# Latent attention on one core: a second bank for the single units, and the turned probabilities in three pieces through two banks

## The chip, the cores and the metric

The kernel runs on one core of a Trainium2 chip. The metric is device time in microseconds of one launch. The engines are PE (TensorE: matmuls and transposes), DVE (VectorE), ACT (ScalarE), POOL (GpSimd) and SP (SyncE, here only DMA). Each works through its own instructions in program order; semaphores tie them together. PE writes its results to PSUM, eight banks of 512 fp32 columns on 128 partitions, from which DVE and ScalarE read.

## The reference, cut to what matters

The whole program is a block of residual layers on x of 4 x 512 x 256: a small mixture with low-rank experts, a first attention, the small mixture again, a mixture of 32 experts, then the **latent attention**, and the mixture of 32 experts once more. The change is in the latent attention alone:

```python
qc = rms_norm(x @ wq_down, q_norm_w)              # 96 columns
q_nope, q_pe = (qc @ wq_up), (qc @ wq_rope)       # 16 heads of 128 and of 64
kvc = rms_norm(x @ wkv_down, kv_norm_w)           # 64 columns
k_nope, v = split(kvc @ wkv_up)                   # 16 heads of 128 and 128
k_rope = x @ wk_rope                              # 64, shared by the heads
q_pe, k_rope = apply_rope(q_pe), apply_rope(k_rope)
scores = einsum('bqhd,bkhd->bhqk', q, k) * scale
probs = softmax(scores + causal_mask)
out = einsum('bhqk,bkhd->bqhd', probs, v).reshape(4, 512, 16 * 128)
return out @ wo
```

## The kernel before, in words

`latent_stage` (L1229 on) handles B = 4 batches of H1 = 16 heads, 64 heads in all, in a software pipeline of STEPS = 66 **steps** S. Each engine has its own loop over S, written by hand; nothing but these loops and the semaphores sets the order. Weights are folded beforehand, so that a head's query has 128 columns and a batch's keys are shared by its heads.

In step S the engines do, in this order:

- **PE** (L1411 on): `scores(S, 0)`, the largest block of the scores of head S (128x512 and a mask product) into its bank of psA; `queries(S + 2)`, the query of the head after next (96x512, L1346) into psU; `scores(S, 1)` and `(S, 2)`, the other blocks; in odd steps from 3 on `values`, the product of the turned probabilities of heads S-3 and S-2 into psO (L1381); a **side unit**, if the step has one; `turn(S - 1)`, which transposes the ten 128x128 blocks of the causal probabilities of head S-1 into psP (L1371).
- **DVE**: `maxima(S, 0)` (L1607); `queries(S + 2)`, which reads the query from psU, multiplies it with the cosines (L1595) and twice with the sines (L1599) and then frees psU; the other maxima; `divide(S, 0..2)`, which turns the exponentials into probabilities (L1614, L1617); then what the step has besides.
- **ScalarE**: the four exponentials of head S (L1469), each group when its maxima are there; in odd steps from 3 on the copy of psO (L1478); the copy of the side unit; the copy of the turned probabilities of head S-1 from psP to prT, 128x1280 in one instruction (L1486).
- **POOL** adds the two parts of the query and stores rows for the experts; SP loads.

The **side units** are single products or transposes of the neighbouring batches: in steps 6 and 7 of a batch (S modulo 16) the turned rows of the next batch ("x"), in 8 and 9 the down product ("d", of which ScalarE also takes the sums of squares, L1447 and L1451), in 13 the turned query rows ("qT"), in 14 and 15 the keys ("k"), and in 2 to 5 the output product of the batch before ("o": sixteen matmuls in L1340 of eight pairs, added to x by DVE in L1662). Queries and side units together are the **single units**. They share one bank, psU, and one semaphore, u_free: unit n begins when unit n-1 has been read out.

DVE's further work lies in fixed steps: added rows of the experts' result (2.04 us in L1563, in steps 0 to 3, 6, 8, 11, 14, 17, 20, 24, 28), the layer norm of the next batch's rows in step 5 of a batch, its norms in step 10, and for the batch before statistics, scales and normal rows in steps 6, 7 and 8. A **bare** step is one with none of all this.

PSUM before: psA three banks (scores), psP three banks, of which 1280 columns are used, psU one, psO one: all eight. The places in psP and prT (BT) and the two places where the banks are given back:

```python
BT = {0: 0, 1: 512, 3: 896, 2: 1024}
...
def unit(key):
    if u_index[key] >= 1:
        pe.wait_ge(u_free, u_index[key])
...
def turn(h):
    if h >= 1:
        pe.wait_ge(pT_ready, h)
    for k, ts in enumerate(BANKS):
        pe.wait_ge(quotient, NBK * h + k + 1)
```

Of the kernel before, what the change touches and what calls it, by code (L numbers as in the profile page):

```python
# [18 lines left out]
P = 128  # L19
# [1209 lines left out]
def latent_stage(nc, block, sem_of, stored, r, ident, la, slot, rows_dram, placed, spare, picks, half_weight, out_dram, reloads, experts_in):  # L1229
# [5 lines left out]
    BT = {0: 0, 1: 512, 3: 896, 2: 1024}  # L1235
    NS = 1280
# [31 lines left out]
    with ExitStack() as ctx:  # L1268
# [3 lines left out]
        def sem(n):  # L1272
# [26 lines left out]
        (dstep, pstep, u_ready, u_free, xn_ready, ss_ready, kv_ready, kn_ready, q_part, q_ready, a_done, nb_ready,  # L1299
         exp_done, quotient, turned, pT_ready, v_done, o_copied, out_done, ptick, xd_ready) = (sem(n) for n in (  # L1300
             "dstep", "pstep", "u_ready", "u_free", "xn_ready", "ss_ready", "kv_ready", "kn_ready", "q_part", "q_ready",
             "a_done", "nb_ready", "exp_done", "quotient", "turned", "pT_ready", "v_done", "o_copied", "out_done",
             "ptick", "xd_ready"))
        outs, OPENS = [psU[:, 0:D], psU[:, D:2 * D], psA[:, 0:D], psA[:, 512:512 + D]], (0, 2, 3)
# [3 lines left out]

        @block.tensor
        def _(pe):  # L1310
            def unit(key):
                if u_index[key] >= 1:
                    pe.wait_ge(u_free, u_index[key])

            def side(key):
                kind, b, n = key
                unit(key)
                if kind == "x":
                    pe.wait_ge(xn_ready, TPB * (b + 1))
                    for j in range(TPB):  # L1320
                        ins = pe.transpose(psU[:, j * P:(j + 1) * P], xn[:, j * D + n * P:j * D + (n + 1) * P], ident[:, :])
                elif kind == "d":
                    for e in range(2):
                        j = 2 * n + e
                        for k in range(KD):
                            ins = pe.matmul(psU[:, e * ND:(e + 1) * ND], xT[:, k * L + j * P:k * L + (j + 1) * P],
                                            la.down[:, k * ND:(k + 1) * ND], start=(k == 0), stop=(k == KD - 1))
                elif kind == "qT":
                    pe.wait_ge(kv_ready, b + 1)
                    for j in range(TPB):  # L1330
                        ins = pe.transpose(psU[0:QR, j * P:(j + 1) * P], qn[:, j * QR:(j + 1) * QR], ident[:, :])
                elif kind == "k":
                    pe.wait_ge(kn_ready, b + 1)
                    o = 0 if n else 64
                    for j in range(TPB):
                        ins = pe.transpose(psU[:, j * P:(j + 1) * P], kn[b % 2][:, j * 192 + o:j * 192 + o + P], ident[:, :])
                else:
                    pe.wait_ge(o_copied, PAIRS * (b + 1))
                    for c in range(PAIRS):
                        ins = pe.matmul(psU[:, 0:D], oT[(b * PAIRS + c) % RING][:, n * P:(n + 1) * P], la.vo[:, c * D:(c + 1) * D],  # L1340
# [3 lines left out]
            def queries(h):  # L1344
                unit(("q", h))
                pe.matmul(psU[:, :], la.qw[:, h % H1 * P:(h % H1 + 1) * P], qT[h // H1 % 2][:, :], start=True,  # L1346
                          stop=True).then_inc(u_ready, 1)

            def scores(h, k):
                if k == 0:  # L1350
                    pe.wait_ge(q_ready, h + 1)
                if k == 0 and h % H1 == 0:
                    pe.wait_ge(u_free, u_index[("k", h // H1, 1)] + 1)
# [10 lines left out]
            def turn(h):  # L1364
                if h >= 1:
                    pe.wait_ge(pT_ready, h)
                for k, ts in enumerate(BANKS):
                    pe.wait_ge(quotient, NBK * h + k + 1)
                    for qt in ts:
                        for kt in range(qt + 1):  # L1370
                            ins = pe.transpose(psP[:, BT[kt] + (qt - kt) * P:BT[kt] + (qt - kt + 1) * P],  # L1371
                                               pr[h % 2][:, AT[qt] + kt * P:AT[qt] + (kt + 1) * P], ident[:, :])
                ins.then_inc(turned, 1)

            def values(g):
                pe.wait_ge(pT_ready, 2 * g + 2)
# [28 lines left out]
            pe.wait_ge(u_free, u_index[("q", 0)])  # L1405
            for h in range(2):
                queries(h)
            for S in range(STEPS):
                if S < HEADS:
                    scores(S, 0)  # L1410
                    if S + 2 < HEADS:  # L1411
# [7 lines left out]
                if 1 <= S <= HEADS:  # L1419
                    turn(S - 1)  # L1420
                if S == HEADS - 1:
                    pe.wait_ge(u_free, len(order))
# [15 lines left out]
        def _(act):  # L1438
            def side(key):
                kind, b, n = key  # L1440
                made(act, key)
                if kind == "x":
                    act.copy(xT[:, n * L:(n + 1) * L], psU[:, :]).then_inc(u_free, 1)
# [391 lines left out]
```

## Time and profile before

| | |
|---|---|
| median of 3 runs | 1489.26 us (1489.18 to 1489.72) |
| profiled execution, its own time | 1499.06 us |
| span of its trace | 1497.0 us |
| mean granted clock of PE in it | 0.934 |
| latent stage within the span | about 700 to 1255 us |
| the 64 turned copies (L1486) | 1.23 us each, from 751.7 to 1244.7 us |

The profiled execution is 9.8 us longer than the median; its durations are used for the working, and sums are made against its own time. In the rows, a time in front is the start in us from the start of the span, then the length in us, the engine and the line. A bracket at the end is how long the engine sat idle before it, and what released it. "x10" is a number of merged instructions. Ends of matmuls are modelled and overlap with the next; the distance of two starts on PE is what a piece costs.

### The profile page before, as it was taken

What the parts mean: (1) busy time and instruction counts of PE and PEld (TensorE: products, weight loads), DVE (VectorE), ACT (ScalarE), POOL (GpSimd) and SP (SyncE); (2) the same over time, 40 slices, a digit from 0 to 9 for tenths busy, and PEclk for the clock granted to TensorE, in tenths of its full rate; (3) what the DMA queues carried; (4) which work ended last, traced back from release to release, by engine and by line L of the source; (5) the groups of instructions that cost most, each with busy time, mean ns of one, the idle gap of its engine ahead of it and who ended that gap; (6) DMA issues with size and microseconds to landing.
All of it is one profiled execution on the core that took longest, in us unless ns stands there. A gap on an engine that the chain in (4) does not pass through costs nothing.

```text
span 1497.0 us, 22302 instructions
## 1 busy us (share of the span) xinstructions
PE 1267.1 (85%) x6633; PEld 816.1 (55%) x6634; DVE 950.7 (64%) x2721; ACT 671.1 (45%) x1706; POOL 502.9 (34%) x495
## 2 busy tenths in 40 slices
PE   6769898898888599998778889889889997899980
PEld 4514243343336578887545455556546556788870
DVE  6786758777756622224498978887897793123227
ACT  2205655555672055553245444453554461255540
POOL 2054040052315645552111211351152153355550
PEclk7959998999999699999999999999999998899995
DMA  7527543073304166554011100020010112344538
GB/s 283 108 25 117 179 85 42 1 150 147 151 19 162 72 231 203 181 166 152 3 54 29 29 1 1 11 103 1 7 36 15 57 43 102 102 157 156 164 124 280
DMA packets 78687, 147.91 MB, mean 99 GB/s; under 512 B 11693, under 2 KB 60014, under 8 KB 75758
## 3 DMA queue, kind: packets, MB, share of 16 engines
q1 hardware_dynamic: 62782, 104.36, 24.8%
q0 software_dynamic: 15360, 41.96, 7.8%
q8 instruction: 60, 0.98, 0.3%
q14 instruction: 53, 0.43, 0.1%
q10 hardware_dynamic: 432, 0.17, 0.0%
HBM read 83.15 MB, written 62.91 MB: 98 GB/s over the span
## 4 chain that ended last, share of the span: by engine, by line
PE 54%; DVE 27%; issue 7%; ACT 6%; POOL 3%; DMA 2%; another core or an unknown queue 0%; SPq 0%; DVEq 0%; POOLq 0%; ACTq 0%
PE m_psG L1164 12%; PE m_psY L1180 5%; DVE a_t L1599 4%; DVE a_mx L852 4%; PE a_psO L456 3%; PE m_psX L1155 3%; DVE a_nb L1607 3%; PE a_psA L1358 3%; PE a_psU L431 3%; PE a_psU L1340 3%; PE a_psW L397 2%; ACT a_pr L1469 2%; POOL rows_dram L166 2%; PE a_psS L442 2%; DVE x L1134 2%
## 5 line engine op out<-in xcount | busy, mean ns | idle before, releaser
L166 POOL DMA_INDIRECT outs_dram<-m_ys,dest x192 | 184.5, 961 | 162.8 <-ACT m_ys L1099 129.8
L1469 ACT ACTIVATE a_pr<-a_psA,a_nb 128x512 f32<-128x512 f32 (+3 forms) x256 | 132.8, 525 | 218.5 <-DVE a_nb L1607 218.0
L1119 DVE TENSOR_TENSOR m_hm<-m_psG,m_sg 128x128 f32<-128x128 f32 x192 | 56.0, 292 | 266.5 <-ACT m_sg L1093 159.2
L852 DVE TENSOR_REDUCE a_mx<-a_psU 128x1 f32<-128x512 f32 x256 | 163.7, 684 | 67.4 <-PE a_psU L431 65.5
L1164 PE MATMUL m_psG<-arena,m_xgT 128*128 x768 | 202.2, 386 | 2.2 <-ACT m_xgT L1087 1.6
L1525 POOL TENSOR_TENSOR a_q<-a_q,a_t 64x512 f32<-64x512 f32 x64 | 80.8, 1263 | 353.3 <-DVEq L1602 329.4
L166 POOL DMA_INDIRECT rows_dram<-a_xd,slot x128 | 139.3, 1089 | 165.3 <-DVE a_xd L146 78.4
L587 ACT ACTIVATE a_P<-a_psS 128x512 f32<-128x512 f32 x256 | 142.7, 597 | 50.8 <-PE a_psS L442 44.7
L1164 PEld LDWEIGHTS m_psG<-arena,m_xgT 128*128 128x128 f32 x768 | 130.6, 190 | 19.0 <-issue 7.1
L1607 DVE TENSOR_REDUCE a_nb<-a_psA 128x1 f32<-128x512 f32 (+3 forms) x256 | 113.3, 485 | 34.9 <-PE a_psA L1360 24.3
L431 PE MATMUL a_psU<-arena 96*128 96x512 bf16 x256 | 106.7, 419 | 32.8 <-DVE a_mx L852 30.7
L1180 PE MATMUL m_psY<-arena,m_hT 128*128 x384 | 115.0, 382 | 0.1
L1087 ACT COPY m_xgT<-m_psX 128x256 f32<-128x256 f32 x192 | 72.4, 378 | 83.5 <-PE m_psX L1155 83.5
L442 PE MATMUL a_psS<-arena 108*128 108x512 bf16 x256 | 97.8, 388 | 9.3 <-ACT a_P L587 7.7
L1358 PE MATMUL a_psA<-arena,a_q 128*128 128x512 f32 (+3 forms) x256 | 91.3, 466 | 16.5 <-ACT a_pr L1469 15.8
L1617 DVE TENSOR_SCALAR a_pr<-a_pr,a_rec 128x512 f32<-128x512 f32 (+3 forms) x256 | 97.1, 401 | 6.8
L1099 ACT COPY m_ys<-m_psY 128x256 f32<-128x256 f32 x192 | 71.5, 372 | 59.0 <-PE m_psY L1180 34.6
L1486 ACT COPY a_prT<-a_psP 128x1280 f32<-128x1280 f32 x64 | 79.1, 1236 | 42.0 <-PE a_psP L1371 41.9
L1358 PE MATMUL a_psA<-a_kT,a_q 128*128 128x512 f32 (+3 forms) x256 | 88.1, 453 | 9.4 <-ACT a_pr L1469 7.6
L1093 ACT ACTIVATE m_sg<-m_psG 128x128 f32<-128x128 f32 x192 | 53.6, 279 | 86.2 <-PE m_psG L1164 75.6
L1599 DVE TENSOR_TENSOR a_t<-a_psU,la_sin 32x512 f32<-32x512 f32 x128 | 87.9, 687 | 1.7
L431 PEld LDWEIGHTS a_psU<-arena 96*128 96x128 bf16 x256 | 25.5, 100 | 111.8 <-DVE a_mx L852 87.9
(270 smaller groups left out, 2319.2 us busy)
## 6 DMA issues: line engine op xcount, KB each, us to landing
m_xg<-rows_dram SPq DMA_DIRECT2D x46, 512.0 KB
arena<-in_mo_w SPq DMA_DIRECT2D x9, 2048.0 KB
arena<-part_dram SPq DMA_DIRECT2D x96, 128.0 KB
arena<-outs_dram SPq DMA_DIRECT2D x16, 512.0 KB, 3.9
rows_dram<-a_P SPq DMA_DIRECT2D x6, 1024.0 KB, 14.1
part_dram<-a_part SPq DMA_DIRECT2D x16, 384.0 KB, 5.3
rows_dram<-arena SPq DMA_DIRECT2D x6, 1024.0 KB, 15.5
m_xg<-outs_dram SPq DMA_DIRECT2D x8, 512.0 KB, 4.6
```

What stands on the lines that cost most here:

```text
L166: pool.indirect_dma_start(out=rows_dram, out_offset=bass.IndirectOffsetOnAxis(ap=slot[:, c:c + 1], axis=0), in_=row, in_offset=None).then_ ...
L431: pe.matmul(psU[n % 2][:, :], QS[0:NT, o + h * L + qt * P:o + h * L + (qt + 1) * P], KS[0:NT, o + h * L:o + (h + 1) * L], start=True, stop ...
L442: pe.matmul(psS[n % 2][:, :], KS[0:KC, o + h * L + kt * P:o + h * L + (kt + 1) * P], QS[0:KC, o + h * L:o + (h + 1) * L], start=True, stop ...
L587: act.activation(Pr[:, o:o + L], psS[c % 2][:, :], ACT.Exp).then_inc(exp_done, 1)
L852: dve.tensor_reduce(mx[g % 2][:, 4 * kt + qt:4 * kt + qt + 1], psU[n % 2][:, :], AX, ALU.max).then_inc(u_free, 1)
L1164: ins = pe.matmul(psG[b % 2][:, 0:2 * INTER], xgT[:, (b % 2) * D + k * P:(b % 2) * D + (k + 1) * P], GU[:, ds(e * (KD * 2 * INTER) + k * 2 ...
L1180: pe.matmul(psY[m % 2][:, 0:D], hT[:, (m % 2) * P:(m % 2 + 1) * P], DW[:, ds(e * D, D)], start=True, stop=True).then_inc(y_done, 1)
L1358: pe.matmul(psA[:, AT[t]:AT[t] + (t + 1) * P], qh[:, t * P:(t + 1) * P], kh[:, 0:(t + 1) * P], start=True, stop=False)
L1469: ins = act.activation(pr[S % 2][:, AT[t]:AT[t] + (t + 1) * P], psA[:, AT[t]:AT[t] + (t + 1) * P], ACT.Exp, bias=nb[S % 2][:, t:t + 1], sc ...
L1599: ins = dve.tensor_tensor(t2[to:to + 32, o:o + L], psU[lo:lo + 32, :], la.sin[lo:lo + 32, :], ALU.mult)
L1607: ins = dve.tensor_reduce(nb[s % 2][:, t:t + 1], psA[:, AT[t]:AT[t] + (t + 1) * P], AX, ALU.max, negate=True)
L1617: ins = dve.tensor_scalar(pt, pt, rec[s % 2][:, t:t + 1], None, ALU.mult)
```

## The change

psP becomes two banks of 512 columns, and the third goes to psU, which is now two banks as well. u_free becomes a pair of semaphores; a unit waits until the one two before it has been read out, and where an engine relied on the order of all units, it now waits for the units it needs (`gone`, `all_gone`). A head is turned in NPC = 3 pieces (key blocks 0; 1 and 3; 2), each into the next of the two banks, and ScalarE copies each by itself (`keep`). Pieces 0 and 1 of head S-1 stand where the whole turning and copy stood, at the end of step S. Piece 2 stands in step S+1: on PE between `scores(S + 1, 0)` and the queries, on ScalarE ahead of the exponentials. Turning waits for all three quotients of its head.

```diff
+    PIECES = (((0,), 0, 512), ((1, 3), 512, 1024), ((2,), 1024, 1280))
+    NPC = len(PIECES)
...
-        psP = ctx.enter_context(nc.psum_tensor("a1_psP", [P, 1536], F32))
-        psU = ctx.enter_context(nc.psum_tensor("a1_psU", [P, 512], F32))
+        psP, psU = ([ctx.enter_context(nc.psum_tensor(f"a1_{n}{i}", [P, 512], F32)) for i in range(2)] for n in ("psP", "psU"))
+        u_free = [sem(f"u_free{i}") for i in range(2)]
...
+        def gone(eng, key):
+            eng.wait_ge(u_free[u_index[key] % 2], u_index[key] // 2 + 1)
...
             def unit(key):
-                if u_index[key] >= 1:
-                    pe.wait_ge(u_free, u_index[key])
+                if u_index[key] >= 2:
+                    pe.wait_ge(free_of(key), u_index[key] // 2)
+                return bank_of(key)
...
-            def turn(h):
-                if h >= 1:
-                    pe.wait_ge(pT_ready, h)
-                for k, ts in enumerate(BANKS):
-                    pe.wait_ge(quotient, NBK * h + k + 1)
-                    for qt in ts:
-                        for kt in range(qt + 1):
-                            ins = pe.transpose(psP[:, BT[kt] + (qt - kt) * P:BT[kt] + (qt - kt + 1) * P],
-                                               pr[h % 2][:, AT[qt] + kt * P:AT[qt] + (kt + 1) * P], ident[:, :])
+            def turn(h, i):
+                m = NPC * h + i
+                if m >= 2:
+                    pe.wait_ge(pT_ready, m - 1)
+                if i == 0:
+                    pe.wait_ge(quotient, NBK * (h + 1))
+                kts, lo, hi = PIECES[i]
+                for kt in kts:
+                    for qt in range(kt, TPB):
+                        o = BT[kt] - lo + (qt - kt) * P
+                        ins = pe.transpose(psP[m % 2][:, o:o + P], pr[h % 2][:, AT[qt] + kt * P:AT[qt] + (kt + 1) * P], ident[:, :])
                 ins.then_inc(turned, 1)
...
             for S in range(STEPS):
                 if S < HEADS:
                     scores(S, 0)
+                if 2 <= S:
+                    turn(S - 2, NPC - 1)
+                if S < HEADS:
                     if S + 2 < HEADS:
                         queries(S + 2)
...
                 if 1 <= S <= HEADS:
-                    turn(S - 1)
+                    for i in range(NPC - 1):
+                        turn(S - 1, i)
...
+            def keep(h, i):
+                m = NPC * h + i
+                _, lo, hi = PIECES[i]
+                act.wait_ge(turned, m + 1)
+                if h >= 2 and i == 0:
+                    act.wait_ge(v_done, h // 2)
+                act.copy(prT[h % 2][:, lo:hi], psP[m % 2][:, 0:hi - lo]).then_inc(pT_ready, 1)
+
             for S in range(STEPS):
+                if S >= 2:
+                    keep(S - 2, NPC - 1)
                 if S < HEADS:
                     if S >= 2:
-                        act.wait_ge(turned, S - 1)
+                        act.wait_ge(turned, NPC * (S - 1))
...
                 if 1 <= S <= HEADS:
-                    h = S - 1
-                    act.wait_ge(turned, h + 1)
-                    if h >= 2:
-                        act.wait_ge(v_done, h // 2)
-                    act.copy(prT[h % 2][:, :], psP[:, 0:NS]).then_inc(pT_ready, 1)
+                    for i in range(NPC - 1):
+                        keep(S - 1, i)
```

How this moves instructions, at two places. First PE at the start of step 59, before (psA scores, psU the query of head 61, psO values; a1_pr holds probabilities):

```order
L1358 MATMUL a1_psA<-a1_kT1,a1_q3 128x512 [waits a1_exp_done,a1_q_ready]
L1360 MATMUL a1_psA<-la_mask,la_identb 128x128
L1346 MATMUL a1_psU<-a1_qT1,la_qw 128x512 [waits a1_u_free]
L1358 MATMUL a1_psA<-a1_kT1,a1_q3 128x384 [waits a1_exp_done]
L1360 MATMUL a1_psA<-la_mask,la_identb 128x128
L1358 MATMUL a1_psA<-a1_kT1,a1_q3 128x128
L1360 MATMUL a1_psA<-la_mask,la_identb 128x128
L1358 MATMUL a1_psA<-a1_kT1,a1_q3 128x256 [waits a1_exp_done]
L1360 MATMUL a1_psA<-la_mask,la_identb 128x128
L1381 MATMUL a1_psO<-a1_prT0,a1_kn1 64x512 [waits a1_o_copied,a1_pT_ready]
```

and of the changed kernel, from the pieces 0 and 1 of head 57 on:

```order
L1392 MATMUL a1_psP1<-ident,a1_pr1 128x128 [waits a1_quotient,a1_pT_ready]
L1392 MATMUL a1_psP1<-ident,a1_pr1 128x128 x3
L1392 MATMUL a1_psP0<-ident,a1_pr1 128x128 [waits a1_pT_ready]
L1392 MATMUL a1_psP0<-ident,a1_pr1 128x128 x3
L1376 MATMUL a1_psA<-a1_kT1,a1_q3 128x512 [waits a1_exp_done,a1_q_ready]
L1378 MATMUL a1_psA<-la_mask,la_identb 128x128
L1392 MATMUL a1_psP1<-ident,a1_pr1 128x128 [waits a1_pT_ready]
L1392 MATMUL a1_psP1<-ident,a1_pr1 128x128
L1363 MATMUL a1_psU1<-a1_qT1,la_qw 128x512 [waits a1_u_free1]
L1376 MATMUL a1_psA<-a1_kT1,a1_q3 128x384 [waits a1_exp_done]
```

Two transposes (piece 2 of head 57) now stand between the first scores and the query, and they wait on pT_ready, which ScalarE's copies raise.

Second ScalarE, from the last exponential of step 58 through step 59, before:

```order
L1469 ACTIVATE a1_pr0,a1_sums0<-a1_psA,a1_nb0 128x256 [waits a1_nb_ready]
L1486 COPY a1_prT1<-a1_psP 128x1280 [waits a1_v_done,a1_turned]
L1469 ACTIVATE a1_pr1,a1_sums1<-a1_psA,a1_nb1 128x512 [waits a1_nb_ready,a1_turned]
L1469 ACTIVATE a1_pr1,a1_sums1<-a1_psA,a1_nb1 128x384 [waits a1_nb_ready]
L1469 ACTIVATE a1_pr1,a1_sums1<-a1_psA,a1_nb1 128x128
L1469 ACTIVATE a1_pr1,a1_sums1<-a1_psA,a1_nb1 128x256 [waits a1_nb_ready]
L1478 COPY arena<-a1_psO 128x512 [waits a1_u_ready,a1_v_done]
L1486 COPY a1_prT0<-a1_psP 128x1280 [waits a1_v_done,a1_turned]
L1469 ACTIVATE a1_pr0,a1_sums0<-a1_psA,a1_nb0 128x512 [waits a1_nb_ready,a1_turned]
```

and of the changed kernel:

```order
L1504 ACTIVATE a1_pr0,a1_sums0<-a1_psA,a1_nb0 128x256 [waits a1_nb_ready]
L1493 COPY a1_prT1<-a1_psP1 128x512 [waits a1_v_done,a1_turned]
L1493 COPY a1_prT1<-a1_psP0 128x512 [waits a1_turned]
L1493 COPY a1_prT1<-a1_psP1 128x256 [waits a1_turned]
L1504 ACTIVATE a1_pr1,a1_sums1<-a1_psA,a1_nb1 128x512 [waits a1_nb_ready,a1_turned]
L1504 ACTIVATE a1_pr1,a1_sums1<-a1_psA,a1_nb1 128x384 [waits a1_nb_ready]
L1504 ACTIVATE a1_pr1,a1_sums1<-a1_psA,a1_nb1 128x128
L1504 ACTIVATE a1_pr1,a1_sums1<-a1_psA,a1_nb1 128x256 [waits a1_nb_ready]
L1513 COPY arena<-a1_psO 128x512 [waits a1_u_ready,a1_v_done]
L1493 COPY a1_prT0<-a1_psP0 128x512 [waits a1_v_done,a1_turned]
L1493 COPY a1_prT0<-a1_psP1 128x512 [waits a1_turned]
L1493 COPY a1_prT0<-a1_psP0 128x256 [waits a1_turned]
```

The one copy of 1280 columns at a step's end became two of 512 there and one of 256 in front of the next step's exponentials.

## Rows read from the trace of the kernel before

**Rows 1.** The page's part 1: busy us, share of the span, instructions
```profile
PE 1267.1 (85%) x6633; PEld 816.1 (55%) x6634; DVE 950.7 (64%) x2721; ACT 671.1 (45%) x1706; POOL 502.9 (34%) x495
```

**Rows 2.** Waits of 760 to 1220 us: engine, line, releaser: us in total, times, longest
```profile
DVE a_nb L1607 <- PE a_psA L1360: 23.9, 17, 2.2
...
DVE x L1662 <- PE a_psU L1340: 13.1, 9, 2.2
...
DVE a_q L1595 <- PE a_psU L1346: 7.7, 25, 0.7
```

**Rows 3.** Timeline of the bare steps 58 and 59: start us, us, engine, line
```profile
1204.92 1.25 ACT L1486 COPY a_prT<-a_psP 128x1280 f32<-128x1280 f32 x1
...
1205.94 0.68 DVE L1595 TENSOR_TENSOR a_q<-a_psU,la_cos 128x512 f32<-128x512 f32 x1
...
1206.23 1.31 PE L1371 MATMUL a_psP<-ident,a_pr 128*128 128x128 f32 x10 [0.22 <-ACT a_prT L1486]
...
1210.31 1.23 ACT L1486 COPY a_prT<-a_psP 128x1280 f32<-128x1280 f32 x1
...
1211.79 2.38 PE L1381 MATMUL a_psO<-a_prT,a_kn 128*64 128x512 f32 x16
...
1211.79 0.68 DVE L1595 TENSOR_TENSOR a_q<-a_psU,la_cos 128x512 f32<-128x512 f32 x1
...
1214.10 1.31 PE L1371 MATMUL a_psP<-ident,a_pr 128*128 128x128 f32 x10
...
1216.19 0.59 ACT L1478 COPY arena<-a_psO 128x512 f32<-128x512 f32 x1
...
1216.65 1.25 ACT L1486 COPY a_prT<-a_psP 128x1280 f32<-128x1280 f32 x1
...
1217.67 0.68 DVE L1595 TENSOR_TENSOR a_q<-a_psU,la_cos 128x512 f32<-128x512 f32 x1
```

**Rows 4.** Timeline of the output steps 34 and 35
```profile
1012.47 3.72 PE L1340 MATMUL a_psU<-la_vo,arena 128*128 128x256 f32 x16 [0.59 <-DVE a_t L1599]
...
1017.12 1.02 PE L1358 MATMUL a_psA<-arena,a_q 128*128 128x512 f32 x2
...
1018.04 1.08 PE L1346 MATMUL a_psU<-arena,la_qw 96*128 96x512 f32 x2
...
1019.15 0.69 DVE L1595 TENSOR_TENSOR a_q<-a_psU,la_cos 128x512 f32<-128x512 f32 x1 [0.22 <-PE a_psU L1346]
...
1022.93 3.72 PE L1340 MATMUL a_psU<-la_vo,arena 128*128 128x256 f32 x16
...
1026.49 1.25 PE L1371 MATMUL a_psP<-ident,a_pr 128*128 128x128 f32 x10
...
1027.58 1.02 PE L1358 MATMUL a_psA<-arena,a_q 128*128 128x512 f32 x2
```

**Rows 5.** The query products on DVE: duration ns min/median/max, first and last start
```profile
L1595 DVE TENSOR_TENSOR a_q<-a_psU,la_cos x64: 673/683/693, 731.8 to 1224.0; 128x512 f32<-128x512 f32 x64
```

**Rows 6.** Copies from PSUM: busy us, mean ns; of 760 to 1220 us, and of the page
```profile
L1478 ACT COPY arena<-a_psO 128x512 f32<-128x512 f32 x29 | 17.1, 590 | 0.0
...
L1087 ACT COPY m_xgT<-m_psX 128x256 f32<-128x256 f32 x192 | 72.4, 378 | 83.5 <-PE m_psX L1155 83.5
```

**Rows 7.** Timeline of ScalarE at the down unit of step 9
```profile
815.23 0.56 ACT L1447 COPY a_dn<-a_psU 128x448 f32<-128x448 f32 x1
...
816.84 1.20 ACT L1486 COPY a_prT<-a_psP 128x1280 f32<-128x1280 f32 x1
```

**Rows 8.** PE after a long wait (timeline), two windows with the granted clock (after the counts)
```profile
880.41 5.41 PE L1340 MATMUL a_psU<-la_vo,arena 128*128 128x256 f32 x16 [2.82 <-DVE a_t L1599]
...
881.00:884.00 3.00, 3.00 (x11) 2.42 (x10) 2.45 (x10) 1.48 (x6) 0.82 (x1) 0.63 0.00 0
...
1192.00:1195.00 3.00, 0.98 (x3) 0.40 (x3) 2.89 (x6) 0.78 (x2) 0.00 (x0) 1.00 0.00 0
```

**Rows 9.** Timeline of the opening: filler matmuls behind the first unit
```profile
711.14 0.83 PE L161 MATMUL a_psO<-ident 128*128 128x128 f32 x6
```

More of the change, by code:

```diff
@@ L1311, in unit @@
             def unit(key):
-                if u_index[key] >= 1:
-                    pe.wait_ge(u_free, u_index[key])
+                if u_index[key] >= 2:
+                    pe.wait_ge(free_of(key), u_index[key] // 2)
+                return bank_of(key)
             def side(key):
                 kind, b, n = key
-                unit(key)
+                bank = unit(key)
                 if kind == "x":
@@ L1320, in side @@
                     for j in range(TPB):
-                        ins = pe.transpose(psU[:, j * P:(j + 1) * P], xn[:, j * D + n * P:j * D + (n + 1) * P], ident[:, :])
+                        ins = pe.transpose(bank[:, j * P:(j + 1) * P], xn[:, j * D + n * P:j * D + (n + 1) * P], ident[:, :])
                 elif kind == "d":
+                    for m in range(2):
+                        gone(pe, ("x", b, m))
                     for e in range(2):
@@ L1344, in queries @@
             def queries(h):
-                unit(("q", h))
-                pe.matmul(psU[:, :], la.qw[:, h % H1 * P:(h % H1 + 1) * P], qT[h // H1 % 2][:, :], start=True,
+                bank = unit(("q", h))
+                if h % H1 == 0:
+                    gone(pe, ("qT", h // H1, 0))
+                pe.matmul(bank[:, :], la.qw[:, h % H1 * P:(h % H1 + 1) * P], qT[h // H1 % 2][:, :], start=True,
                           stop=True).then_inc(u_ready, 1)
@@ L1352, in scores @@
                 if k == 0 and h % H1 == 0:
-                    pe.wait_ge(u_free, u_index[("k", h // H1, 1)] + 1)
+                    for n in range(2):
+                        gone(pe, ("k", h // H1, n))
                 if h >= 1:
@@ L1441, in side @@
                 made(act, key)
+                bank = bank_of(key)
                 if kind == "x":
-                    act.copy(xT[:, n * L:(n + 1) * L], psU[:, :]).then_inc(u_free, 1)
+                    act.copy(xT[:, n * L:(n + 1) * L], bank[:, :]).then_inc(free_of(key), 1)
                 elif kind == "d":
@@ L1446, in side @@
                         act.wait_ge(kn_ready, b)
-                    act.copy(dn[:, 2 * n * ND:(2 * n + 2) * ND], psU[:, 0:2 * ND]).then_inc(u_free, 1)
-                    act.wait_ge(u_free, u_index[key] + 1)
+                    act.copy(dn[:, 2 * n * ND:(2 * n + 2) * ND], bank[:, 0:2 * ND]).then_inc(free_of(key), 1)
+                    gone(act, key)
                     for j in (2 * n, 2 * n + 1):
@@ L1453, in side @@
                 elif kind == "qT":
-                    act.copy(qT[b % 2][:, :], psU[0:QR, :]).then_inc(u_free, 1)
+                    act.copy(qT[b % 2][:, :], bank[0:QR, :]).then_inc(free_of(key), 1)
                 elif kind == "k":
@@ L1594, in queries @@
                     dve.wait_ge(a_done, NBK * (h - 3))
-                dve.tensor_tensor(q[h % 4][:, :], psU[:, :], la.cos[:, part * L:(part + 1) * L], ALU.mult)
+                bank = bank_of(("q", h))
+                dve.tensor_tensor(q[h % 4][:, :], bank[:, :], la.cos[:, part * L:(part + 1) * L], ALU.mult)
                 o = (h // 2 % 2) * L
@@ L1598, in queries @@
                     to = lo + 32 if lo == 64 * part else lo - 32
[L1599 to L1601 removed]
+                    ins = dve.tensor_tensor(t2[to:to + 32, o:o + L], bank[lo:lo + 32, :], la.sin[lo:lo + 32, :], ALU.mult)
+                ins.then_inc(free_of(("q", h)), 1)
+                gone(dve, ("q", h))
                 dve.sem_inc(q_part, 1)
```

37 lines of the change are left out of this document (20 added, 17 removed).

## The prediction

> **What bounds the kernel now.** I read the page first, then the waits of the latent stage, then its timeline step by step, because one step repeats 64 times. The page has PE at 85% and DVE at 64% [rows 1], but these are means over stages with different limits. In the latent stage (about 700 to 1255 us) DVE alone is late only where the waits name it: 23.9 us before the first row maxima, 13.1 us before the output sum, 7.7 us before the query product, 44.7 us together [rows 2]. That is the most that better supply of DVE can give.
>
> I measure a step from one start of the query product on DVE (L1595) to the next; there are 64 of them, the last at 1224.0 [rows 5]. Two kinds of step matter.
>
> A **bare step** (no added rows, no single unit beside the query) is DVE's own length: 1205.94 to 1211.79 and on to 1217.67, 5.85 and 5.88 us [rows 3]. DVE has no gap there, PE is ahead, and ScalarE writes the turned probabilities when it has finished the exponentials, 4.37 us (even step) and 4.40 us (odd step) after the query product began [rows 3].
>
> A **step with an output unit** (eight products and their sum, twelve such steps) is PE's: from 1017.12 to 1027.58, 10.46 us without a gap, of which 3.56 are the unit (1022.93 to 1026.49) and 2.31 the values (1211.79 to 1214.10), which only odd steps have [rows 3, 4]. PE alone would then need 10.46 - 2.31 = 8.15 us in an even one and 10.46 - 3.56 = 6.90 in an odd step without the unit. The even ones take 8.8, because the unit waits 0.59 us for the only bank until DVE has read the query out of it [rows 4]. Once that wait was 2.82 us, and the granted clock of the following 3 us was 0.63 [rows 8].
>
> **The change part by part.**
>
> *Second bank for the single units.* It removes the 0.59 us in even output steps. I take 8.15 for 8.80 to 8.82 in steps 34, 36, 50, 52: 2.65 us. Step 18 has the long wait and the low clock; it took 10.49, now 8.15: 2.3. Step 20 adds rows on DVE and falls from 8.86 to DVE's own 8.33 (5.88, 2.04 for the added rows, 0.42 for the sum): 0.5. After the two layer norms beside output units (steps 21, 37) the query waited behind DVE's sum, 0.61 each: 1.2. Step 40 had a down unit waiting 2.57: 0.55. **Together -7.2 us.** Plain odd output steps gain nothing, they are PE's work from end to end.
>
> *The third piece of turning, and where it stands.* This is what I expect to decide. Head h is turned in pieces 0, 1, 2 through banks alternating. Piece 2 reuses the bank of piece 0, so it waits until ScalarE has copied piece 0. ScalarE copies piece 0 of head S-1 only at the end of its step S, behind the exponentials of head S (and the output copy in odd steps). And on PE piece 2 stands ahead of the queries of the next step, which DVE wants right away. Before, nothing that early on PE waited for this copy: only the next turning did, a whole step later.
> The sum for a bare step: the exponentials end 4.40 after the query product [rows 3]; copy of 128x512 out of PSUM 0.59 [rows 6]; to PE's start 0.06 (1204.92 + 1.25 = 1206.17, PE at 1206.23 [rows 3]); two transposes 0.22 (ten take 1.09, 1026.49 to 1027.58 [rows 4]); from the start of the query matmuls to DVE's product 1.11 (1018.04 to 1019.15 [rows 4]). That is 6.38 us from one query product to the next, where DVE alone needs 5.86: +0.52 after each even step. In odd steps the output copy adds 0.46 (1216.19 to 1216.65 [rows 3]), so 6.84; but by then PE has lost its lead, and its own 6.90 is longer: +1.03.
> Steps in which DVE has more work hide all of this: with a layer norm step 5 took 11.41 us, with the norms step 10 took 10.06, with added rows steps 1 to 3 took 7.8. What is left (the periods named here are those between the 64 starts that [rows 5] count):
> - bare even steps 4, 12, 16, 32, 44, 48, 58: 7 x 0.52 = 3.6.
> - bare odd steps 49, 57, 59: 3 x 1.03; 27, 33, 43 took 6.18 to 6.33, now 6.90: 1.9. Together 5.0.
> - steps with a unit that ScalarE copies ahead of piece 0. Odd steps 13, 29, 45 (turned queries): 6.67 to 7.40, 2.2. Even 30, 46 (keys): 6.19 to 6.85, 1.3. Odd 15, 31, 47 wait for the new batch's keys anyway: 0.3. Step 7: 0.7. Down units hold ScalarE 1.61 us (815.23 to 816.84 [rows 7]): steps 8, 9, 25, 41 +0.2, +0.9, +0.6, 0.
> **Together +14.8 us.**
>
> *Three copies for one.* 0.59 + 0.59 + 0.38 [rows 6] for 1.23 [rows 3]: 0.3 us more on ScalarE per head. The copies of pieces 1 and 2 end before the next exponential can begin; apart from the wait above I count nothing. If ScalarE were full at that point, it would be 0.33 x 22 steps in which it sets the pace, 7 us; that is the upper bound of this term, nothing the lower.
> The Trainium skill, page "Perfetto Trace Analysis", section "Optimizing Scalar/DVE Operations", gives about 51 ns of access overhead to each ScalarE operation on PSUM and advises larger operations where an engine is full. By its figure two more copies would be 0.10 us per head and that upper bound 2.2 us (an estimate from that page); the rows give 0.33, and the rows decide.
>
> *Turning no longer starts on the first quotient,* but on all three. PE is behind DVE's quotients wherever it is the bound, and ahead elsewhere; nothing.
>
> *Opening.* The seven units before the loop alternate banks. Each is followed by filler matmuls as long as the copy (0.83 against 0.59 [rows 9, 6]), so this gives under 0.5; counted at nothing.
>
> *End.* In step 63 PE waits once more for the copy ahead of the last scores, 1.0 us, and the last piece of head 63 is turned after the 24 products of step 64, so that its copy (0.38) and two handovers lie bare before the last values: 0.6. **+1.6 us.**
>
> Sum: 14.8 - 7.2 + 1.6 = **+9.2 us**. The profiled execution took 1499.06 and would take 1508.3; the median of the runs is 9.8 us (0.7%) lower, 1489.26, and would be **1498.5**. Differences under about 0.2%, 3 us, cannot be told from none.
>
> **Rivals.**
> *The banks do what double buffering promises.* If ScalarE's copy of piece 0 did not hold PE, the second bank would also end the idle time of steps 7, 9, 25, 30, 31 and 41 (7.8 us, each down to DVE's length), with no +14.8 and no +1.6: 1489.3 - 7.2 - 7.8 = **1474.3**. For it: the long waits on the single bank are real [rows 4, 8]. Against: order of ScalarE's queue; the copy sits behind exponentials that end 4.4 us into a step of 5.9 [rows 3]. The Trainium skill, page "Perfetto Trace Analysis", section "Matmuls", advises just this rotation, so that the evacuation of one group overlaps the matmuls of the next. By that rule this rival's time would come out; the trace shows the evacuating engine busy with earlier work.
> *No measurable difference.* The wait costs half of what I reckon (7 us), for instance because PE gets ahead again in the long steps and keeps that lead longer: 1489.3 - 7.2 + 7.4 + 0.8 = **1490.3**.
> *The clock falls too.* In my account PE idles about 1.7 us in each even bare step, ahead of piece 2. After 2.82 us idle the clock was 0.63 for 3 us, between its levels of 1.2 and 2.4 GHz, and the sixteen matmuls of the output unit took 5.41 us instead of 3.72 [rows 8, 4]. If that comes in eight of the steps in which PE is now the bound, at 1.5 us each, it is 12 us more: **1510**. Against: in 1192 to 1195 PE was busy for 0.98 of 3 us and the clock stayed at 1.00 [rows 8].
>
> **How the numbers follow.** My forecast has 0.72 of the chance (1493 to 1504: terms of 15 and 7 us with errors of a quarter); the rotation that works 0.10; no difference 0.09; the clock 0.09. Leaving out the first rival and the far half of the last, the range is 1490 to 1508. Faster is the first rival and a bit of the second, 0.11; within 0.2% (1486.3 to 1492.2) the second and the edge of mine, 0.10; slower the rest, 0.79.
>
> **What would show it.** In bare steps of the changed kernel: queries on PE (now L1363) start 0.3 us after ScalarE's first piece copy (L1493) ends; DVE waits some 0.5 us before the query product; pairs of steps take 13.3 us instead of 11.7. PE's wait for ScalarE's copy ahead of the transposes (0.22 us at 1206.23 before [rows 3]) becomes one of its longest in total. In output steps the wait on the query's bank is gone and even ones take 8.15. If PE shows no wait at piece 2 in bare steps, the account of the slowdown is wrong; if the clock is under 0.9 where it was 1.0, the last rival holds.

## The result, and the profile after

The changed kernel took 1507.76 us in the median of 4 runs (1506.54 to 1510.61), beside 1489.49 us for the kernel before on the same chip: a ratio of 1.011, 95% interval 1.0092 to 1.0128. It is 18.3 us slower, about 1.2%; forecast were +9.2 us. The way and the range (1490 to 1508) hold, the range by its last 0.24 us alone: one of the four runs lies outside it, and the median outside the 1493 to 1504 that the forecast itself was given. Of the ten runs in the experiment "The same copy twice, with a bank for each piece", one took 2781.76 us where the others took 1485.83 to 1490.81; the ratio there leaves it out, and the median would be 1487.80 without it.

The page's part 1, and the groups of the turning in part 5, of the changed kernel (line numbers are those of the changed kernel: L1392 is the transpose, L1493 its copy, L1363 the queries, L1628 the query product, L1376 scores, L1355 the output unit, L1401 the values):

```profile
PE 1260.0 (84%) x6634; PEld 811.8 (54%) x6634; DVE 951.7 (63%) x2721; ACT 686.9 (46%) x1834; POOL 501.5 (33%) x495
...
L1392 PE MATMUL a_psP<-ident,a_pr 128*128 128x128 f32 x640 | 95.9, 281 | 65.1 <-ACT a_prT L1493 65.1
...
L1493 ACT COPY a_prT<-a_psP 128x512 f32<-128x512 f32 (+1 forms) x192 | 93.1, 524 | 44.9 <-PE a_psP L1392 42.6
```

PE and DVE do the same work as in [rows 1]; ScalarE has 128 instructions and about 16 us more. What is new is the 65.1 us behind the first group: PE standing ahead of a transpose for ScalarE's copy. The waits of the latent stage (760 to 1220 us) say the same:

```profile
PE a_psP L1392 <- ACT a_prT L1493: 58.8, 33, 3.3
...
DVE a_nb L1640 <- PE a_psA L1378: 25.9, 19, 2.8
DVE a_q L1628 <- PE a_psU L1363: 20.3, 33, 1.6
...
DVE x L1695 <- PE a_psU L1355: 8.7, 4, 2.2
```

DVE's wait for the query product grew from 7.7 us in 25 waits to 20.3 us in 33 [rows 2]. DVE's for the output product fell from 13.1 us in nine waits [rows 2] to 8.7 in four. PE's wait for the single unit bank ahead of the output products, which the kernel before has in the same stretch, is gone:

```profile
PE a_psU L1340 <- DVE a_t L1599: 6.1, 6, 2.8
```

The timeline of the bare step 58 and the start of step 59, which answers to [rows 3]:

```profile
1210.11 1.51 ACT L1493 COPY a_prT<-a_psP 128x512 f32<-128x512 f32 x3
...
1210.78 0.44 PE L1392 MATMUL a_psP<-ident,a_pr 128*128 128x128 f32 x2 [0.53 <-ACT a_prT L1493]
1211.05 1.02 PE L1363 MATMUL a_psU<-a_qT,la_qw 96*128 96x512 f32 x2
...
1212.12 0.69 DVE L1628 TENSOR_TENSOR a_q<-a_psU,la_cos 128x512 f32<-128x512 f32 x1 [0.90 <-PE a_psU L1363]
...
1216.05 0.47 ACT L1504 ACTIVATE a_pr<-a_psA,a_nb 128x256 f32<-128x256 f32 x1
...
1216.49 1.49 ACT L1493 COPY a_prT<-a_psP 128x512 f32<-128x512 f32 x3
...
1217.14 0.44 PE L1392 MATMUL a_psP<-ident,a_pr 128*128 128x128 f32 x2 [1.69 <-ACT a_prT L1493]
...
1217.41 1.02 PE L1363 MATMUL a_psU<-a_qT,la_qw 96*128 96x512 f32 x2
...
1218.47 0.69 DVE L1628 TENSOR_TENSOR a_q<-a_psU,la_cos 128x512 f32<-128x512 f32 x1 [0.41 <-PE a_psU L1363]
```

Read it from the bottom. DVE's query product at 1218.47 waited 0.41 us for the queries, which began at 1217.41 behind the two transposes of piece 2, which PE began at 1217.14 after standing 1.69 us, until the first of ScalarE's three copies (from 1216.49, the first 0.59 us long) had emptied the bank, and that copy stood behind the last exponential. The period is 6.35 us where it was 5.85.

The output steps 34 and 35, which answer to [rows 4]:

```profile
1015.32 3.67 PE L1355 MATMUL a_psU<-la_vo,arena 128*128 128x256 f32 x16
...
1021.91 0.69 DVE L1628 TENSOR_TENSOR a_q<-a_psU,la_cos 128x512 f32<-128x512 f32 x1 [0.39 <-PE a_psU L1363]
...
1025.68 3.72 PE L1355 MATMUL a_psU<-la_vo,arena 128*128 128x256 f32 x16
```

The unit of the even step starts with no wait (0.59 us before), and the step went from 8.82 to 7.96 us (1013.95 to 1021.91).

**The balance by steps.** The periods between the starts of the query products from step 0 to step 61 add up to 484.57 us before and to 499.10 us after. Losses are 24.4 us, gains 9.8. From the last query product to the values of the last heads it was 25.8 us before and is 27.6 now. That makes 16.3 us. The profiled executions differ by only 1507.57 - 1499.06 = 8.5 us, because that of before was a long one: 484.57 of its time in these steps where a second execution has 482.52 (first experiment), and some 8 us more in the stages around. With 482.52 the difference is 18.4 us, that of the medians.

### The profile page after: what moved, and what is told of

Read it like the earlier page. It is cut to its first block, busy times and chain, and to the rows that moved or that the text cites. A ratio compares the mean times of both kernels' runs of the same rounds, so it can differ in the third digit from the quotient of the medians.

```text
span 1505.5 us, 22448 instructions
## 1 busy us (share of the span) xinstructions
PE 1260.0 (84%) x6634; PEld 811.8 (54%) x6634; DVE 951.7 (63%) x2721; ACT 686.9 (46%) x1834; POOL 501.5 (33%) x495
## 4 chain that ended last, share of the span: by engine, by line
PE 54%; DVE 27%; ACT 8%; issue 6%; POOL 3%; DMA 2%; SPq 0%; DVEq 0%; POOLq 0%; ACTq 0%
PE m_psG L1164 11%; PE m_psY L1180 5%; DVE a_mx L852 4%; DVE a_t L1632 4%; PE a_psA L1376 4%; ACT a_pr L1504 3%; PE a_psO L456 3%; DVE a_nb L1640 3%; PE m_psX L1155 3%; PE a_psU L1363 3%; PE a_psU L431 3%; PE a_psO L1401 3%; POOL rows_dram L166 3%; PE a_psP L1392 2%; PE a_psU L1355 2%
## 5 line engine op out<-in xcount | busy, mean ns | idle before, releaser
L1392 PE MATMUL a_psP<-ident,a_pr 128*128 128x128 f32 x640 | 95.9, 281 | 65.1 <-ACT a_prT L1493 65.1
L1392 PEld LDWEIGHTS a_psP<-ident,a_pr 128*128 128x128 f32 x640 | 71.5, 143 | 100.1 <-ACT a_prT L1493 92.9
L1493 ACT COPY a_prT<-a_psP 128x512 f32<-128x512 f32 (+1 forms) x192 | 93.1, 524 | 44.9 <-PE a_psP L1392 42.6
L1376 PE MATMUL a_psA<-arena,a_q 128*128 128x512 f32 (+3 forms) x256 | 96.1, 487 | 5.9 <-POOL a_q L1557 2.8
L1376 PE MATMUL a_psA<-a_kT,a_q 128*128 128x512 f32 (+3 forms) x256 | 91.1, 465 | 0.9 <-ACT a_pr L1504 0.5
```

Source lines behind the costliest of these rows:

```text
L1376: pe.matmul(psA[:, AT[t]:AT[t] + (t + 1) * P], qh[:, t * P:(t + 1) * P], kh[:, 0:(t + 1) * P], start=True, stop=False)
L1392: ins = pe.transpose(psP[m % 2][:, o:o + P], pr[h % 2][:, AT[qt] + kt * P:AT[qt] + (kt + 1) * P], ident[:, :])
```

## The experiments

Three theories were to be told apart. **(W)**, the forecast: PE stands at piece 2 until ScalarE has copied piece 0, and DVE's query stands behind PE. **(C)**, its rival: three copies instead of one (and turning that starts only on all three quotients) cost ScalarE, and so everyone, the time. **(K)**, the second rival: the waits let the granted clock fall, and PE pays in the steps in which it is the bound. All ratios are to the kernel before on the same chip, with 95% intervals; periods are in us per step.

### The kernel before, once more

No edit.

> The kernel before, unchanged, for a second profile. The profiled execution of before took 1499 us where its other runs took 1489; every theory expects 1489 +- 1 for the median, and I expect the ten microseconds of that one profile to lie outside the bare steps (which stay 5.86 us), in places where the granted clock fell. If its bare steps differ instead, my reading of the steps was built on an odd execution.

1490.86 us, ratio 0.9995 (0.9979 to 1.0012). Periods as before, but step 18 took 8.80 instead of 10.49 and step 40 7.14 instead of 8.54; and, against my expectation, one bare step was longer, step 57 with 6.74 instead of 5.88, at a granted clock of 0.83. How long step 18 is changes from one execution to the next: of the six profiled executions here whose single units share one bank, three have it at 10.44 to 10.49 and three at 8.59 to 8.80, while step 40 takes 8.22 to 8.62 in five of them. My -2.3 for step 18 thus counted on time that half of these executions don't have.

### Piece 2 behind all scores

```diff
-                if 2 <= S:
-                    turn(S - 2, NPC - 1)
                 if S < HEADS:
                     if S + 2 < HEADS:
                         queries(S + 2)
                     for k in range(1, NBK):
                         scores(S, k)
+                if 2 <= S:
+                    turn(S - 2, NPC - 1)
```

> One edit of the changed kernel: PE turns piece 2 behind the scores instead of ahead of the queries, all waits kept. Theory W (PE stands at piece 2 until ScalarE has copied piece 0, and DVE's query stands behind it): bare steps fall from 6.35 and 6.86 to about 5.9, no low clock in them, and the time to 1474 to 1482, faster than both kernels. Rival C (the cost is the third copy on ScalarE and turning that starts only on all quotients): within 3 us of the changed kernel, 1505 to 1508.

1487.86 us, 0.9958 (0.9939 to 0.9976): faster than before, but not by as much as the 1474 to 1482 that I had expected. Bare steps are 5.85 to 5.88 again, but for steps 32 and 48 (6.80 and 6.74) and 59 (6.03); the even output steps take 7.89 to 7.96, the odd ones without added norms 10.99 to 11.00 where the changed kernel has 10.41; and the periods add up to 476.60 us. ScalarE still copies three times. (W) holds, (C) does not. In the profiled execution the end took 34.0 us instead of 27.6, for a reason in one place:

```profile
1224.49 0.37 ACT L1493 COPY a_prT<-a_psP 128x256 f32<-128x256 f32 x1 [4.18 <-remote]
...
1224.91 4.54 PE L1401 MATMUL a_psO<-a_prT,a_kn 128*64 128x512 f32 x16 [3.78 <-ACT a_prT L1493]
```

ScalarE stood still 4.18 us with nothing in the profile that it waited for. PE stood with it, and the sixteen value products that came next took 4.54 us for 2.38 [rows 3], at a granted clock of 0.50. What stopped ScalarE is open.

### The changed turning, the single units in one bank

```diff
-                if u_index[key] >= 2:
-                    pe.wait_ge(free_of(key), u_index[key] // 2)
+                if u_index[key] >= NU:
+                    pe.wait_ge(free_of(key), u_index[key] // NU)
```

with NU = 1, and the same in `gone`, `all_gone` and the choice of the bank.

> The changed kernel with the single units back in one bank (the second is left unused), turning as changed. This is the turning alone. W and C both expect the changed kernel plus what the second bank gives: even output steps back from 7.96 to about 8.6, 7 us or more in all, so 1514 to 1518. If it is the same as the changed kernel, the second bank gives nothing and all of my -7.2 is wrong.

1516.43 us, 1.0154 (1.0125 to 1.0183); most bare steps 6.35 and 6.91 (at a low clock step 49 took 8.54, 43 7.96 and 57 7.79), even output steps 8.77, step 20 8.86, steps 21 and 37 12.46 and 12.45. Periods 505.80 for 499.10: the second unit bank gives 6.7 us within the changed order, where I had 7.2.

### A bank for each piece

NU = 1 as before this, psP of three banks, and the wait three pieces back:

```diff
-                if m >= 2:
-                    pe.wait_ge(pT_ready, m - 1)
+                if m >= NP_:
+                    pe.wait_ge(pT_ready, m - NP_ + 1)
```

> As one_unit_bank, but the three pieces have a bank each, so piece 2 waits for the copy of the previous head's piece 2, made a step earlier. Three copies, three turnings, the same order. W: the wait ahead of the queries is gone and bare steps are 5.9 again, time that of before within 3 us, 1488 to 1493. C: no better than one_unit_bank, 1510 or more.

1496.49 us, 1.0027 (1.0008 to 1.0046). The order on every engine is that of the changed kernel, and the copies are still three; only the bank of piece 2 is its own:

```profile
1203.31 1.37 ACT L1494 COPY a_prT<-a_psP 128x512 f32<-128x512 f32 x3
...
1206.50 0.39 PE L1393 MATMUL a_psP<-ident,a_pr 128*128 128x128 f32 x2
...
1206.72 1.02 PE L1364 MATMUL a_psU<-a_qT,la_qw 96*128 96x512 f32 x2
```

PE reaches piece 2 without a wait, and bare steps are 5.85 to 5.88 but for step 32 (6.89). On the same chip that is 20 us less than with two banks for the pieces (1516.43). What is left over before, 0.3%, bounds (C) in this order: 4 us, by the interval 1 to 7, not 18.

### Piece 2 between the queries and the smaller scores

```diff
-                if 2 <= S:
-                    turn(S - 2, NPC - 1)
-                if S < HEADS:
-                    if S + 2 < HEADS:
-                        queries(S + 2)
+                if S + 2 < HEADS:
+                    queries(S + 2)
+                if 2 <= S:
+                    turn(S - 2, NPC - 1)
+                if S < HEADS:
                     for k in range(1, NBK):
                         scores(S, k)
```

> One edit of the changed kernel: on PE piece 2 stands between the queries and the smaller scores, so that DVE's query no longer stands behind it, and piece 2 is still early enough for ScalarE to copy it ahead of the values (behind the scores it was not: output steps with values took 11.0 there). Theory W: bare steps near 5.9, odd output steps 10.4, even ones 7.96; 476 - 2.4 = about 474 us over the 61 steps, and 1483 to 1487 in all. If it is not better than behind the scores (1488), the copy ahead of the values was not what cost those 0.6 us.

1475.82 us beside 1483.94 of the kernel before on its chip: 0.9951 (0.9927 to 0.9975), faster than the kernel before, and by the ratios faster than the changed one. Periods 474.92 us, bare steps 5.85 to 5.92 but for three odd ones of 6.34 to 6.37. The odd output steps take 10.46 for the 11.0 that they took with piece 2 behind all scores; in the whole the two places can't be told apart (476.60 us there, 474.92 and, in the repeat, 476.68 here). Where piece 2 still waits, DVE does not (from the repeat on another chip, step 61):

```profile
1207.87 1.08 PE L1363 MATMUL a_psU<-a_qT,la_qw 96*128 96x512 f32 x2
...
1208.85 1.49 ACT L1493 COPY a_prT<-a_psP 128x512 f32<-128x512 f32 x3
...
1209.49 0.44 PE L1392 MATMUL a_psP<-ident,a_pr 128*128 128x128 f32 x2 [0.55 <-ACT a_prT L1493]
...
1210.34 0.68 DVE L1628 TENSOR_TENSOR a_q<-a_psU,la_cos 128x512 f32<-128x512 f32 x1
```

The wait on the bank is there as in the changed kernel, 0.55 us at 1209.49 (0.53 at 1210.78 there, in step 58), but the queries were issued 1.6 us ahead of it.

### Filler matmuls in PE's wait

```diff
+                if 3 <= S < HEADS and S % 2 and (side_unit(S - 1) or "-")[0] != "o":
+                    pe.wait_ge(exp_done, NBK * (S - 1) + 2)
+                    stay_warm(pe, psA[:, 512:1024], ident, 3)
                 if 2 <= S:
                     turn(S - 2, NPC - 1)
```

> The changed kernel with three filler matmuls (0.83 us) on PE in the wait ahead of piece 2 in odd steps whose predecessor has no output unit; the wait itself is unchanged. Theory K (PE's short waits, one after the other, let the granted clock fall, and where PE is the bound this costs): the long ones among the bare steps (7, 9, 27, 28, 49, 59, which took 9.3, 9.1, 8.0, 8.8, 8.5, 8.5 us) fall to 7.4, 8.5, 6.9, 7.8, 6.9, 6.9, and the time by about 7 us, to 1500 or so. If the time stays at 1507 or rises, the fillers only cost what they take, and something else made those steps long.

1495.24 us, 1.0091 (1.0061 to 1.0121); periods 495.94, 3.2 less than in the changed kernel, where I had expected about 7. In the whole time the intervals overlap with those of the changed kernel, so that the effect is read from the steps. Steps 7, 27, 49 and 59 went from 9.29, 7.96, 8.54, 8.54 to 7.34, 6.86, 6.91, 6.91: the lengths that (W) gives at the full clock, 6.3 us gained. But 3.2 were given back in steps 43, 56 and 57, which became long instead (7.95, 7.89 and 8.24, at granted clocks of 0.77, 0.73 and 0.84). Step 9 (9.13, at a clock of 1.00) and step 28 (8.75) stayed long, against what I had expected. The granted clock of the same stretch, of the changed kernel and of this one (the number ahead of the last two):

```profile
791.00:801.00 10.00, 10.00 (x47) 5.51 (x46) 6.39 (x16) 5.28 (x14) 1.27 (x1) 0.78 0.18 53
```

```profile
791.00:801.00 10.00, 9.23 (x56) 5.91 (x55) 8.15 (x18) 5.24 (x15) 1.27 (x1) 1.00 0.19 55
```

Step 7 is long because its clock is low, which is (K). With fillers in half of the waits the clock fell at other places, and some 3 us of net gain are left.

Step 28 has another cause, which lies on DVE. It adds rows there in four instructions, merged in one line; first the kernel before, then the changed one:

```profile
975.20 2.04 DVE L1563 SCALAR_TENSOR_TENSOR x<-arena,weight,x 128x256 f32<-128x256 f32 x4
```

```profile
974.60 2.92 DVE L1595 SCALAR_TENSOR_TENSOR x<-arena,weight,x 128x256 f32<-128x256 f32 x4
974.80 1.40 POOL L1557 TENSOR_TENSOR a_q<-a_q,a_t 64x512 f32<-64x512 f32 x1 [1.52 <-DMA rows_dram<-a_xd,slot]
```

One of the four began while POOL's addition ran, and took 1.37 us instead of 0.49. This is so in all five profiled executions with piece 2 ahead of the queries and two banks for the pieces (2.92 to 2.98 us for the four), also where the clock was at 1.00 throughout (with the first copy twice, below: 2.92 us, step 28 8.71); and with piece 2 behind the queries step 28 took 7.80 though its clock was 0.78. So the wait shifts DVE against POOL, and that costs 0.9 us here.

### The first copy twice

```diff
+                if i == 0:
+                    act.copy(again[h % 2][:, :], psP[m % 2][:, 0:512])
                 act.copy(prT[h % 2][:, lo:hi], psP[m % 2][:, 0:hi - lo]).then_inc(pT_ready, 1)
```

> The changed kernel with piece 0 copied twice by ScalarE, first into a buffer that nobody reads (0.47 us more behind the exponentials, ahead of the copy that PE waits for). W: bare even steps grow by the whole copy, 6.35 to 6.82, odd ones from 6.86 to 7.3, units of the batches alike, some 22 steps: 8 to 12 us more than the changed kernel, 1516 to 1520. If ScalarE's copy is not on the path, no change.

1519.04 us, 1.0257 (1.0213 to 1.0302). The bare even steps 12, 48 and 58 took 6.83 to 6.85, 0.48 more than in the changed kernel: each added copy lies in the path at nearly its full start-to-start length (1220.34 to 1220.81, 0.47 us). But odd bare steps took 7.34 to 8.56 and step 9 10.92, so the periods add up to 517.43, 18.3 more than in the changed kernel, where I had expected 8 to 12; that 1519 lies within my 1516 to 1520 is because this chip is faster (before: 1483.94). PE's waits had become longer, with the clock after them (ahead of step 57's query product):

```profile
1221.47 0.44 PE L1393 MATMUL a_psP<-ident,a_pr 128*128 128x128 f32 x2 [2.94 <-ACT a_prT L1496]
...
1222.60 1.34 PE L1377 MATMUL a_psA<-a_kT,a_q 128*128 128x384 f32 x2
```

The scores of 0.81 us took 1.34.

### The same copy twice, with a bank for each piece

> The same second copy in the kernel with a bank for each piece (1496 us), where nothing early waits for piece 0. W: its bare steps stay 5.86 to 5.9 and the time within 3 us of 1496. Rival C (ScalarE is full there, whoever waits): the same 8 to 12 us more as in first_copy_twice.

1488.05 us, 1.0035 (1.0015 to 1.0056), beside 1.0027 without the second copy. The same added instruction, 64 times 0.47 us of ScalarE from start to start, costs 18 us where PE waits for it and 2 us (periods 489.54 for 487.48) where it does not. That settles (C) for this order: ScalarE has room.

### The three kernels that matter, side by side

The changed kernel again; the order of "Piece 2 between the queries and the smaller scores" again; and this order with NU = 1.

> The changed kernel itself, once more, on one chip with the two runs beside it. Both theories: as measured first, 1.011 times the time before (1.009 to 1.013), bare pairs of steps 13.3 us. If the fallen clock in steps 7, 9, 27, 28, 49 and 59 is a habit of the kernel, the same steps are long again (7: 9.3, 9: 9.1, 28: 8.8, 49 and 59: 8.5 us); if it was an accident of that execution, they stand at 7.4, 8.5, 7.8 and 6.9, and the time is 1.006.

> Piece 2 turned behind the queries, as before: theory of the wait 0.995 of the time before (0.993 to 0.998), and 0.984 of the changed kernel on the same chip. Were the earlier result an accident of its chip, 1.000.

> Piece 2 behind the queries, and the single units in one bank again: what is left is only the turning in three pieces. If the gain over before (0.995) is the second unit bank's, as I now reckon, this takes 1.000 of the time before (0.998 to 1.002), with even output steps at 8.8 us instead of 8.0. If the gain comes from turning in pieces and two banks give nothing once the wait is gone, it takes 0.995, as its neighbour.

| on one chip | median us | ratio to before | periods |
|---|---|---|---|
| changed kernel | 1511.16 | 1.0104 (1.0084 to 1.0124) | 499.02 |
| piece 2 behind the queries | 1487.01 | 0.9956 (0.9937 to 0.9976) | 476.68 |
| the same, one unit bank | 1496.27 | 1.0003 (0.9989 to 1.0017) | 485.62 |

Turning in three pieces is worth nothing by itself (third row); the second unit bank gives 0.47%, 9.3 us; the place of two transposes costs 1.6%, 24 us. In the third row the wait on the single bank is back, 0.37 us in step 34 and more elsewhere:

```profile
1005.88 3.72 PE L1356 MATMUL a_psU<-la_vo,arena 128*128 128x256 f32 x16 [0.37 <-DVE a_t L1633]
```

Nine us are more than the 6.7 in the changed order. Part of that is steps 6 and 7: here the second bank takes step 7 from 7.39 to 5.87, to DVE's length, and step 6 from 8.31 to 7.82, while in the changed order step 7 got longer with it, 9.29 for 7.35, at the low clock. The rest lies in steps that change from one execution to the next (step 13: 8.42 at a clock of 0.80 with one bank, 6.79 with two), and is not shown to be the bank's.

The repeat of the changed kernel has steps 7, 9, 27 and 28 long again (9.33, 9.13, 7.96, 8.82) but 49 and 59 at 6.91; in their place 41, 43 and 57 are longer (10.65, 7.42 and 7.74). The sum is the same within 0.1 us. So for 49 and 59 it was that execution; the first four are long in both. One and the same wait in the two executions, with the window of 1 us that follows; first the changed kernel as profiled at first:

```profile
1217.14 0.44 PE L1392 MATMUL a_psP<-ident,a_pr 128*128 128x128 f32 x2 [1.69 <-ACT a_prT L1493]
...
1221.14 2.81 PE L1401 MATMUL a_psO<-a_prT,a_kn 128*64 128x512 f32 x16
...
1220.00:1221.00 1.00, 1.00 (x5) 0.53 (x3) 0.86 (x2) 0.00 (x0) 0.21 (x1) 0.50 0.00 0
```

then its repeat:

```profile
1218.32 0.44 PE L1392 MATMUL a_psP<-ident,a_pr 128*128 128x128 f32 x2 [1.69 <-ACT a_prT L1493]
...
1221.13 2.38 PE L1401 MATMUL a_psO<-a_prT,a_kn 128*64 128x512 f32 x16
...
1220.00:1221.00 1.00, 1.00 (x8) 0.72 (x6) 0.99 (x2) 0.12 (x2) 0.00 (x0) 1.00 0.00 0
```

From the end of the wait to the values it took 4.00 us in the one, at a granted clock of 0.50 in the window shown, and 2.81 in the other, at 1.00.

## Why the prediction was right, and where its size was off

The mechanism was right and its size too small. The median fell into the range at its edge, nearer to the 1510 of the clock's rival (chance 0.09) than to the 1498.5 of the forecast: that it is inside is luck, since the range reached to 1508 only by half of that rival.

**The third piece's wait** was the right step and decided the sign. Each of its parts was found: bare even steps 6.34 to 6.36 (forecast 6.38), odd ones at the full clock 6.86 to 6.91 (6.90), turned queries 7.33 (7.40), keys 6.84 (6.85), queries on PE 0.3 us after the copy's end, DVE waiting 0.4 to 0.9 us. Moving two transposes takes all of it away, a third bank does too. Sized +14.8, the losses measured +24.4 from step to step. By my own groups: bare even steps 4.3 for 3.6; odd ones 9.2 for 5.0; steps with turned queries or keys (13, 29, 45, 30, 46) 3.3 for 3.5; steps 15, 31, 47 1.2 for 0.3; step 7 2.6 for 0.7; down units 2.7 for 1.7; steps 28 and 6, counted at nothing, 1.1.

**The term that failed is the clock,** which I had kept in a rival and out of the sum. Of the excess of 9.6 us, 6.2 lie in steps with a low clock in which PE's work is late: 7 (1.9 over its forecast), 27 (1.1), 49 and 59 (1.6 each). Their granted clocks were 0.79, 0.80, 0.81 and 0.80, all four 1.00 in the kernel before, which is what I had named as the sign of the last rival. The rest is the down units (step 9 took 9.13 for 8.5, step 41 9.13 for 8.5, both at a granted clock of 1.00), the keys' steps, where ScalarE holds the copy back longer than I had reckoned, step 32 (6.87 for 6.38, and 6.53 in the repeat), and step 28, where 0.9 us are the added rows beside POOL, which no term of mine had. After the longest wait the clock is seen best, in windows of the changed kernel across the end of step 27:

```profile
964.00:967.00 3.00, 0.21 (x1) 0.22 (x2) 2.82 (x11) 2.71 (x9) 2.48 (x4) 0.84 0.00 0
967.00:970.00 3.00, 3.00 (x6) 1.44 (x6) 1.43 (x4) 1.27 (x4) 2.05 (x5) 0.50 0.00 0
970.00:973.00 3.00, 3.00 (x13) 2.31 (x12) 2.66 (x7) 0.77 (x3) 2.39 (x3) 0.52 0.24 87
```

PE stood 3.27 us until 966.79, and then worked 6 us at half clock, 1.2 GHz, so that DVE waited 1.56 us for the query. My argument against the rival was one row, a stretch with PE a third busy and the clock at 1.00 [rows 8]. It showed one mild case; the row beside it, 2.82 us idle and a clock of 0.63, was nearer to what came. I had also taken every wait for 1.7 us, while steps with a unit that ScalarE copies make it 3.3. The rival was "eight steps at 1.5 us, 12 us more, 1510"; it was four at 1.1 to 1.9 in one execution, and partly others in the next.

**The second unit bank** was -7.2, measured -9.8 against the profiled execution: even output steps 7.96 (8.15 forecast), step 18 7.03 for 8.15, steps 21 and 37 -1.4, step 20 -0.7, step 40 -0.6. Against the second execution of before the gains add up to 7.7, and taking the second bank alone away costs 6.7. The size was right for the order that it came with, and low for a better one, where it is 9.3.

**Three copies** at nothing: 0.0% (at most 0.2) with piece 2 behind the queries and one unit bank, 0.3% (0.1 to 0.5) with a bank for each piece. The 0.33 us per head behind my upper bound was misread: 0.59 + 0.59 + 0.38 are durations, and copies overlap, starting 0.47 us apart (1220.34 and 1220.81). Where nothing comes between them the three take 1.37 us for 1.25, 0.12 more; the 1.49 of the changed kernel hold the third copy's wait for its transposes. The opening counted at nothing: step 0's query product began at 734.27 us, in the two executions of before at 739.45 and 733.21, so that nothing can be told. **End** +1.6: measured +1.8, and +3.2 in the repeat (29.0 us).

**The first rival,** banks that work as double buffering (1474), failed at its condition, that the copy of piece 0 doesn't hold PE. With piece 2 behind the queries the gain is there, 7 to 9 us of the 15 that this rival had; what it lacks are steps 9, 25, 31 and 41, which stay at 7.5, 7.8, 7.8 and 8.2, and the end, 27.6 us there too.

**From the profiled execution to the median** I moved the forecast by -9.8 us; the second execution of before bore that out (1488.45), but 2 us of it lay inside the stage (484.57 and 482.52), so that the gain was counted too high by these.

## What to carry to other kernels

A buffer that alternates is worth what its emptier lets it be worth. Before giving a producer fewer places, look at where the emptying instruction stands in its own engine's queue, and at what stands behind the producer's wait; moving the waiting instruction behind the one that the bottleneck needs (here two transposes of 0.22 us) changed the sign of this edit. And price a new wait on TensorE twice: its length, and the slower clock of the steps behind it if these are TensorE's own.

## What the hardware showed that I had not expected

A wait of 1.69 us ahead of the same instruction was followed by a granted clock of 0.50 in one execution and of 1.00 in another. Around the wait of 3.27 us ahead of PE's step 28 the clock fell in both executions of the changed kernel and in that with the fillers; after one of 3.26 us, ahead of step 44 (its end at 1100.63), it stayed at 1.00 in the first execution. The Trainium skill, page "TensorE: Matmul & The Clock Gate", Part 1, calls the chip's observation of TensorE free-running, independent of when the program starts; the two executions agree with that, though they don't prove it. For whoever prices a wait, it means a mean over executions, not the one figure of a trace.

An instruction of DVE's added rows that begins while POOL adds the query's parts takes 1.37 to 1.43 us, in five of five cases; the others take at most 0.60 us in all thirteen profiled executions of this stage. Why is not shown here. For the reader of a trace it means that a shift between two engines that wait for nothing of each other can have a price too.

The 4.18 us in which ScalarE stood without a releaser, in one profiled execution, is unexplained.
